# A centred head weight made on chip, the layers' result turned as it is, and the offset's row left in the tail

## The chip, the cores and the metric

The kernel runs on one core of one Trainium2 chip. Its time is the device time of one execution, in microseconds (us); the profile shows the same program in one execution of its own, as a span from the first to the last instruction. The engines are PE (TensorE: matmuls, with the weight loads kept apart as PEld), DVE (VectorE), ACT (ScalarE), POOL (GpSimd) and SP (SyncE, which here issues all DMAs). Each runs its own instructions in the order in which they are written and meets the others at semaphores.

## The reference

A small vision tower in three parts. Two images of 32 x 128 x 128 are cut into 256 patches each and embedded in 128 features. Two layers follow, each an attention with factored softmaxes and a feed-forward of 512 with GELU, all with layernorms. A last layernorm and a head of 128 x 192 give the tokens of the second and third parts, a linear attention and a feed-forward of 768 at width 192. What the change touches is the last norm and the head:

```
return _ln(x, lnf_g, lnf_b) @ head_w + head_b     # _ln: (x - mean) * rsqrt(var + eps) * g + b
...
h = h + attn(_layernorm(h))
h = h + ffn(_layernorm(h))
```

Written out for a token, h = rstd * ((x - mean) * g) @ head_w + (b @ head_w + head_b). The part (x - mean) can be taken on either side of the product: (x - mean) * g @ head_w equals x @ (g * head_w - m), where each row of m is the mean over the 128 features of g * head_w, since mean is a mean over the same features.

## The kernel before

All weights lie in SBUF and are loaded once by SP in a written order; nothing is tiled over DMA. A token tile is 128 tokens, and each image has two (`TILES`). Tensors x, h, xn, yT and so on exist once for each image (x0, x1), eight PSUM banks are shared under several names (`KB`, `QB`, `VB`, `SB_`, `CB`). The work of each engine is an order written out by hand in one block for each engine, so that what stands behind a waiting instruction waits too.

The start embeds image 0 and then image 1 (`conv`). Then come four steps s = 0 to 3, step s being the attention of layer s // 2 for image s % 2, with the feed-forward of the step before it folded in: on PE, the q, k and v products, `turn_k`, the feed-forward, `context`, `turn_q`, `context_out`, `attend`. After step 3 comes the tail: the head of image 0, the feed-forward of image 1's second layer (its norm is LN2(1)), and then the second and third parts of both images, interleaved.

A norm goes over five engines' turns: DVE takes moments (`bn_stats`, `bn_aggr` into mv), POOL makes rstd (`rsqrt`, L1356), DVE writes xn (`norm_apply`, L823), PE transposes xn into a bank, and ACT or DVE applies gain and offset on the way to SBUF as yT. The matrices are split in a high and a low part, so yT_lo (the rest of yT after rounding) is one more subtraction, `norm2_low`, on POOL (L1363) or, for the tail's LN2(1), on DVE (L853). `next_rsqrt` is `rsqrt` followed by `after_norm`, which holds POOL until DVE has written both tiles of xn.

The last norm, LNF, takes no rstd in xn: `normf_centre` (L830) on DVE writes x - mean, `turn_norm` transposes it, `normf` (L1200) on ACT multiplies by the gain, `head` (L501) multiplies by headw, and `h_from_head` (L967) on DVE multiplies by rstd and adds headb. headb is one row, repeated over 128 partitions: `offset_through_head` (L509) on PE, then `head_bias` (L836) on DVE. On PE the tail begins

```
attend(1, 1, 1)
turn_norm(0, LNF, CB)
offset_through_head()
head(0)
turn_norm(1, LN2(1), QB[0])
ff1_begin(1, 1)
ff1_end(1, 1)
turn_norm3(0, LN3, T3)
```

and `ff1_end` starts with a wait for image 1's yT_lo. LN3 is the norm ahead of the linear attention. `mix_masks` (L889) and `mix_sum` (L894) on DVE combine masks for the weights of the third part, in step 0; POOL first uses their result at `mix_fc(0)`, in step 2 (at 49.50 us of the profile).

Of the kernel before, what the change touches and what calls it, by code (L numbers as in the profile page):

```python
# [26 lines left out]
ALU = mybir.AluOpType  # L27
# [3 lines left out]
P = 128  # L31
# [4 lines left out]
D = 128  # L36
# [50 lines left out]
def build(nc, small, embed0, patches1, qkv_w, rest_w, rows, mix, fc_w, proj_w, head_w, aqkv_w, aout_w, out):  # L87
    with ExitStack() as ctx:
# [63 lines left out]
        headb = sb("headb", [P, E])  # L152

# [107 lines left out]
        headb_done, headb_ready = sem("headb_done"), sem("headb_ready")  # L261
# [27 lines left out]
        XN = {n: TILES * n for n in range(LN4 + 1)}  # L289
# [51 lines left out]
        def _(pe):  # L341
# [155 lines left out]
            def head(i):  # L497
                pe.wait_ge(loaded["head"], 16)
                pe.wait_ge(norm_ready[i], 2 * LAYERS + 1)
                for t in range(TILES):  # L500
                    mm = nc.tensor.matmul(HB[i][:, t * E:(t + 1) * E], yT[i][:, t * P:(t + 1) * P], headw[:],  # L501
                                          start=True, stop=True)
                mm.then_inc(head_done, 1)


            def offset_through_head():
                pe.wait_ge(loaded["head"], 16)
                offset = col("lnf_b").to_broadcast([P, P])
                nc.tensor.matmul(KB[1][:, 0:E], offset, headw[:], start=True, stop=True).then_inc(headb_done, 1)  # L509
# [147 lines left out]
            for t in range(TILES):  # L657
                conv(1, 13, KCONV, (t,))
            turn_q(0, 0, 0)
# [6 lines left out]
            for s in range(1, STEPS):  # L666
# [5 lines left out]
                pe.wait_ge(tile0_ready[i], 2 * l + 1)  # L672
                q_part(l, i, 0, "high")
# [39 lines left out]
                turn_q(l, i, 1)  # L713
                attend(l, i, 0)
# [4 lines left out]
            turn_norm(0, LNF, CB)  # L719
            offset_through_head()  # L720
            head(0)
# [15 lines left out]
            turn_norm(1, LNF, CB)  # L737
# [65 lines left out]
        def _(dve):  # L803
# [23 lines left out]
            def normf_centre(i):  # L827
                for t in range(TILES):
                    dve.wait_ge(moments[i], 2 * TILES * LNF + TILES + t + 1)
                    nc.vector.tensor_scalar(xn[i][:, t, 0:D], x[i][:, t, :], mv[i][:, t, 0:1], None,  # L830
                                            ALU.subtract).then_inc(xn_ready[i], 1)

            def head_bias():
                dve.wait_ge(headb_done, 1)
                dve.wait_ge(loaded["rows"], 16)
                nc.vector.tensor_tensor(headb[:], KB[1][:, 0:E], rows_sb[:, ROW["head_b"]:ROW["head_b"] + E],  # L836
                                        ALU.add).then_inc(headb_ready, 1)
# [125 lines left out]
            def h_from_head(i, t):  # L963
                dve.wait_ge(headb_ready, 1)
# [79 lines left out]
            mix_alpha()  # L1044

# [8 lines left out]
            for s in range(STEPS):  # L1054
# [26 lines left out]
                else:  # L1081
# [12 lines left out]
                    mix_masks()  # L1094
                context_scaled(l, i, 1)
                if s < STEPS - 1:
                    norm_apply(1 - i, LN1((s + 1) // 2), x[1 - i], D)
                else:
                    normf_centre(0)
                if s == 0:  # L1100
                    mix_sum()
# [9 lines left out]

            norm_apply(1, LN2(1), x[1], D)
            head_bias()
            for t in range(TILES):
                h_from_head(0, t)
            norm_stats(0, LN3, h[0], E, h_ready[0], 1, 1)
            norm2_low(1, 1)
            norm_apply(0, LN3, h[0], E)
# [9 lines left out]
            normf_centre(1)  # L1128
# [48 lines left out]
        def _(act):  # L1177
# [175 lines left out]
        def _(pool):  # L1353
# [227 lines left out]
```

## Time and profile before

| what | us |
|---|---|
| median of 3 runs | 122.61 |
| lowest and highest | 121.50, 123.34 |
| the profiled execution, its time | 121.18 |
| its span | 119.4 |
| PE busy in the span | 111.2 (93%) |
| DVE, ACT, POOL busy | 83.7, 64.8, 52.3 |
| span up to the head of step 1, steps 1 to 3 | 31.7; 14.2, 14.25, 14.05 |
| between the last step and the tail (74.2 to 80.5) | 6.3, of which PE busy 4.85 |

The profiled execution's time is 1.78 above its span, and it lies 1.43 under the median of the runs. Busy time of PE is that of matmuls in flight, so that a 93% busy PE need not be at its peak. TensorE's granted clock is full in all 40 slices of the page. A row of the timeline gives the start in us from the span's start, the length, the engine, the line of the kernel, what is written and read, and how many instructions of that kind were merged; the bracket at its end gives the idle time of the engine just ahead of it and what ended that.

### The profile page before, as it was taken

The page shows a single profiled execution, that of the slowest core. Times are in us where ns is not written, and L with a number is a line of the kernel's source. Part 1 is how long each engine was busy: PE and PEld are TensorE (multiplying, and loading weights), DVE is VectorE, ACT ScalarE, POOL GpSimd, SP SyncE. Part 2 cuts the span into 40 slices and gives each one's busy share as a digit, 9 for nine tenths or more (in the row PEclk, how much of TensorE's full clock was granted, in tenths as well). Part 3 has the DMA queues.
Part 4 walks back from the last instruction along what each step waited for, and adds up shares of the span by engine and source line. Part 5 has one row for each costly group of instructions (what it writes and reads, how often), then busy time and mean ns, then how long its engine had stood idle before and what let it go on. Part 6 is the DMA issues. An engine that isn't in the chain of part 4 may idle for free.

```text
span 119.4 us, 2459 instructions
## 1 busy us (share of the span) xinstructions
PE 111.2 (93%) x916; PEld 100.5 (84%) x916; DVE 83.7 (70%) x246; ACT 64.8 (54%) x148; POOL 52.3 (44%) x62
## 2 busy tenths in 40 slices
PE   6979999999999999999999999689958999999991
PEld 6969998987888989889897998379856979999990
DVE  5000376998999978999699998769896897264202
ACT  4000075464869967899679975257515283521520
POOL 0000108268049970697425999436806860022000
PEclk9999999999999999999999999999999999999999
DMA  3999999996900000000000000000000000000202
GB/s 106 341 409 419 397 367 414 419 407 192 370 2 0 0 5 3 0 0 5 0 0 0 0 5 0 5 0 0 5 0 0 0 0 0 5 0 0 66 0 66
DMA packets 4011, 11.97 MB, mean 100 GB/s; under 512 B 448, under 2 KB 1568, under 8 KB 4000
## 3 DMA queue, kind: packets, MB, share of 16 engines
q1 hardware_dynamic: 4000, 11.82, 26.2%
q8 instruction: 7, 0.11, 0.4%
q14 instruction: 4, 0.03, 0.1%
HBM read 11.43 MB, written 0.39 MB: 99 GB/s over the span
## 4 chain that ended last, share of the span: by engine, by line
PE 52%; DMA 12%; POOL 12%; DVE 7%; issue 6%; SPq 6%; ACT 3%; POOLq 0%; DVEq 0%
DMA restw<-in_rest_w 12%; PE bank L523 7%; PE bank L351 7%; PE bank L601 6%; PE bank L357 5%; PE bank L492 4%; PE bank L458 4%; PE bank L430 3%; PE bank L448 3%; POOL rstd L1356 3%; POOL aqkvw_lo L1417 2%; SPq L304 2%; PE bank L586 2%; SPq L310 2%; POOL qn L1375 2%
## 5 line engine op out<-in xcount | busy, mean ns | idle before, releaser
L1356 POOL TENSOR_TENSOR rstd<-mv,minus_half 128x2 f32<-128x2 f32 x14 | 10.6, 758 | 39.8 <-DVE mv L812 39.7
L1214 ACT ACTIVATE qkvw_hi<-qkvw 128x512 fp32r<-128x512 f32 x6 | 3.6, 626 | 12.9 <-DMA qkvw<-in_qkv_w 12.9
L1219 ACT ACTIVATE kexp<-bank,nkmax 128x256 f32<-128x256 f32 x16 | 7.4, 473 | 3.8 <-DVE nkmax L898 3.8
L1375 POOL TENSOR_TENSOR qn<-q,rqsum 128x512 f32<-128x512 f32 x8 | 8.3, 1042 | 2.4 <-DVE rqsum L921 2.4
L374 PEld LDWEIGHTS bank<-embed_sb 128*128 128x128 f32 x64 | 7.9, 200 | 1.0 <-DMA embed_sb<-in_embed 0.9
L601 PE MATMUL bank<-projw_raw,patches_sb 128*128 128x192 f32 x48 | 8.8, 326 | 0.0
L374 PE MATMUL bank<-embed_sb 128*128 128x128 f32 x64 | 8.1, 285 | 0.8 <-DMA embed_sb<-in_embed 0.8
L458 PE MATMUL bank<-cw,qT 128*128 128x128 f32 x64 | 8.8, 282 | 0.0
L374 PE MATMUL bank<-embed_sb,patches_sb 128*128 128x128 f32 x64 | 8.7, 278 | 0.0
L458 PEld LDWEIGHTS bank<-cw,qT 128*128 128x128 f32 x64 | 7.8, 192 | 0.8 <-issue 0.8
L374 PEld LDWEIGHTS bank<-embed_sb,patches_sb 128*128 128x128 f32 x64 | 8.1, 191 | 0.4
L1268 ACT ACTIVATE patches_sb<-bank,fcb 128x256 f32<-128x256 f32 x12 | 4.9, 471 | 6.3 <-PE bank L523 6.3
L492 PE MATMUL bank<-restw,hid 128*128 128x128 f32 x64 | 8.1, 280 | 0.0
L601 PEld LDWEIGHTS bank<-projw_raw,patches_sb 128*128 128x128 f32 x48 | 7.7, 190 | 0.0
L492 PEld LDWEIGHTS bank<-restw,hid 128*128 128x128 f32 x64 | 7.4, 192 | 0.2
L1417 POOL TENSOR_TENSOR qkvw_lo<-qkvw,qkvw_hi 128x512 fp32r<-128x512 f32 x5 | 6.3, 1281 | 2.9 <-DVE yT_lo L848 2.9
L1241 ACT ACTIVATE qT<-bank 128x512 f32<-128x512 f32 x8 | 4.8, 600 | 4.5 <-PE bank L448 4.5
L1247 ACT ACTIVATE hid<-bank,small_sb 128x256 f32<-128x256 f32 x16 | 6.3, 474 | 1.5 <-PE bank L351 1.5
L1370 POOL TENSOR_TENSOR xb<-x,rows_sb 128x256 f32<-128x256 f32 x8 | 5.9, 735 | 2.7 <-DVE xn L823 1.7
L357 PE MATMUL bank<-qkvw_hi,yT_lo 128*128 128x512 f32 x16 | 6.9, 432 | 0.0
L1179 ACT ACT_TABLE_LOAD x5 | 6.4, 1283 | 0.8 <-PEq L1573 0.7
L823 DVE TENSOR_SCALAR xn<-x,mv,rstd 128x128 f32<-128x128 f32 x16 | 4.8, 342 | 2.8 <-POOL rstd L1356 2.8
(152 smaller groups left out, 331.0 us busy)
## 6 DMA issues: line engine op xcount, KB each, us to landing
embed_sb<-in_embed SPq DMA_DIRECT2D x2, 768.0 KB, 6.6
restw<-in_rest_w SPq DMA_DIRECT2D x2, 768.0 KB, 15.1
patches_sb<-in_patches SPq DMA_DIRECT2D x2, 512.0 KB, 9.2
embed_sb<-in_embed SPq DMA_DIRECT2D x2, 384.0 KB, 8.0
qkvw<-in_qkv_w SPq DMA_DIRECT2D x3, 256.0 KB, 9.7
patches_sb<-in_patches SPq DMA_DIRECT2D x1, 768.0 KB, 12.0
qkvw<-in_qkv_w SPq DMA_DIRECT2D x1, 768.0 KB, 16.1
embed_sb<-in_fc_w SPq DMA_DIRECT2D x1, 768.0 KB, 6.2
```

The costliest lines, as they stand in the source:

```text
L351: mm = nc.tensor.matmul(dst, left(w, n), right(y, n), **ends(which, n, chunks))
L357: mm = nc.tensor.matmul(dst, left(y, n), right(w, n), **ends(which, n, chunks))
L374: mm = nc.tensor.matmul(EMB[i][t][:, 0:D], patches[:, t * P:(t + 1) * P], embed_sb[:, c, 0:D], start=(c == 0), stop=(c == KCONV - 1))
L458: mm = nc.tensor.matmul(VB[t][:, 0:D], qT[i][:, t, c * P:(c + 1) * P], cw[i][:, c, :], start=(k == 0), stop=(k == PAIRS - 1))
L492: mm = nc.tensor.matmul(banks[t][:, 0:D], hid[i][:, c, t * P:(t + 1) * P], ff2w(l, c), start=(c == 0), stop=(c == FC - 1))
L523: mm = nc.tensor.matmul(dst, left, right, start=(which == "high" and k == 0), stop=(which == "low" and k == len(order) - 1))
L601: mm = nc.tensor.matmul(QB[t][:, 0:E], hid3[i][:, c, t * P:(t + 1) * P], projw[:, c, :], start=(c == 0), stop=(c == HC - 1))
L1179: nc.scalar.activation(table_in[:], minus_half[:], func).then_inc(table_loaded, 1)
L1219: nc.scalar.activation(kexp[i][:, c, :], KB[c // 2][:, (c % 2) * TOKENS:(c % 2 + 1) * TOKENS], ACT.Exp, bias=nkmax[i][:, c:c + 1], accum_o ...
L1356: nc.gpsimd.tensor_tensor(rstd[i][:], mv[i][:, :, 1], minus_half[:], ALU.pow).then_inc(rstd_ready[i], 1)
L1375: nc.gpsimd.tensor_tensor(qn[i][:, t, :].rearrange("p (h d) -> p h d", h=HEADS), q[i][:, t, :].rearrange("p (h d) -> p h d", h=HEADS), rqs ...
L1417: nc.gpsimd.tensor_tensor(lo, raw, hi.bitcast(F32), ALU.subtract).then_inc(split_lo[name], 1)
```

## The change

There is a new buffer headc [128, 192], and a new column gain_mean = lnf_g / 128, made on DVE in the start. At the end of step 0 a new matmul on PE, `head_mean`, multiplies gain_mean, repeated over 128 columns, by headw and leaves the mean row in bank KB[0]; DVE's `head_centred` forms headc = headw * lnf_g - that row. `mix_masks` moves behind the `norm_apply` of step 0, `mix_sum` behind the one of step 1. The layers' result x is transposed without centring (`turn_x`), for image 0 inside the last step, ahead of its `attend`, for image 1 where the centred one was turned; `normf` on ACT is a plain copy. `head(0)` follows the last `attend` at once, and the offset's row comes behind it. On DVE, `head_bias` and both `h_from_head(0, t)` now stand ahead of `norm_apply(1, LN2(1))`, and `norm2_low(1, 1)` stands behind `norm_apply(0, LN3)`. On POOL `rsqrt(0, LNF)` moves ahead of two weight operations, and the second layer's bias of image 1 behind the rstd of LN3.

```diff
+            def head_mean():
+                pe.wait_ge(loaded["head"], 16)
+                pe.wait_ge(gain_mean_ready, 1)
+                pe.wait_ge(ktok_ready[0], 1)
+                nc.tensor.matmul(KB[0][:, 0:E], gain_mean[:].to_broadcast([P, P]), headw[:],
+                                 start=True, stop=True).then_inc(head_rows_done, 1)
+            def turn_x(i, dst):
+                for t in range(TILES):
+                    pe.wait_ge(x_new[i], TILES * (LAYERS - 1) + t + 1)
+                    mm = nc.tensor.transpose(dst[:, t * P:(t + 1) * P], x[i][:, t, :], ident)
+                mm.then_inc(turned[i], 1)
...
             for t in range(TILES):
                 conv(1, 13, KCONV, (t,))
+            head_mean()
             turn_q(0, 0, 0)
...
+                if s == 1:
+                    pe.wait_ge(head_rows_ready, 1)
                 q_part(l, i, 0, "high")
...
                 turn_q(l, i, 1)
+                if s == STEPS - 1:
+                    turn_x(0, CB)
                 attend(l, i, 0)
...
             attend(1, 1, 1)
-            turn_norm(0, LNF, CB)
+            head(0)
             offset_through_head()
-            head(0)
             turn_norm(1, LN2(1), QB[0])
...
-            turn_norm(1, LNF, CB)
+            turn_x(1, CB)
...
+            def head_centred():
+                dve.wait_ge(head_rows_done, 1)
+                nc.vector.scalar_tensor_tensor(out=headc[:], in0=headw[:], scalar=col("lnf_g"), in1=KB[0][:, 0:E],
+                                               op0=ALU.mult, op1=ALU.subtract).then_inc(head_rows_ready, 1)
...
-                nc.scalar.activation(yT[i][:], bankof[:, 0:TOKENS], ACT.Copy, scale=col("lnf_g")).then_inc(norm_ready[i], 1)
+                nc.scalar.activation(yT[i][:], bankof[:, 0:TOKENS], ACT.Copy).then_inc(norm_ready[i], 1)
...
             mix_proj_bias()
             normalise_q(1, 1, 1)
             add_bias(1, "out_b", 1, x_new[1], TILES)
+            rsqrt(0, LNF)
             aqkv_low_part(0)
             mix_fc_bias()
-            rsqrt(0, LNF)
-
-            next_rsqrt(1, LN2(1))
+
+            rsqrt(1, LN2(1))
+            next_rsqrt(0, LN3)
             add_bias(1, "ff2_b", 1, x_mid[1], TILES * LAYERS)
-            next_rsqrt(0, LN3)
```

Three places show how instructions stand (the lines in the second listing of each are those of the changed kernel). In the listings a row is one instruction or a run of equal ones: line, operation, what is written and read, and the columns. First DVE at the end of step 0, before and after (x1 is the embedded image 1, bank6 in the row of cw holds the attention's output weights times the context):

```order
L812 BN_AGGR mv1<-stats1 128x2 x2
L889 TENSOR_TENSOR weighted<-mix_sb,alpha 128x594
L948 TENSOR_SCALAR cw<-bank6,rksum0 128x128
L823 TENSOR_SCALAR xn1<-x1,mv1,rstd1 128x128 x2
L894 TENSOR_REDUCE coef<-weighted 128x66
L955 TENSOR_TENSOR x0<-bank4,xb0 128x128
L842 TENSOR_SCALAR yT1_hi<-bank6,small_sb 128x128
```

```order
L834 BN_AGGR mv1<-stats1 128x2 x2
L852 SCALAR_TENSOR_TENSOR headc<-headw,small_sb,bank0 128x192
L970 TENSOR_SCALAR cw<-bank6,rksum0 128x128
L845 TENSOR_SCALAR xn1<-x1,mv1,rstd1 128x128 x2
L911 TENSOR_TENSOR weighted<-mix_sb,alpha 128x594
L977 TENSOR_TENSOR x0<-bank4,xb0 128x128
L864 TENSOR_SCALAR yT1_hi<-bank6,small_sb 128x128
```

The masks' product made room for headc and went behind xn1, and the masks' sum left step 0; it stands behind xn0 of step 1.

Next PE from the last turn of q in step 3 to the first product of the feed-forward, before and after (bank4 and bank5 take the attention of the two tiles):

```order
L448 MATMUL bank3<-small_sb,qn 128x128 x4
L458 MATMUL bank4<-cw,qT 128x128 x4
L458 MATMUL bank5<-cw,qT 128x128 x4
L387 MATMUL bank7<-small_sb,xn0 128x128 x2
L509 MATMUL bank1<-headw,small_sb 128x192
L501 MATMUL bank0<-headw,yT0 128x192 x2
L387 MATMUL bank2<-small_sb,xn1 128x128 x2
L351 MATMUL bank7<-yT1_hi,ff1w1_hi 128x256
L351 MATMUL bank6<-yT1_hi,ff1w1_hi 128x256
```

```order
L451 MATMUL bank3<-small_sb,qn 128x128 x4
L526 MATMUL bank7<-small_sb,x0 128x128 x2
L461 MATMUL bank4<-cw,qT 128x128 x4
L461 MATMUL bank5<-cw,qT 128x128 x4
L504 MATMUL bank0<-headc,yT0 128x192 x2
L512 MATMUL bank1<-headw,small_sb 128x192
L390 MATMUL bank2<-small_sb,xn1 128x128 x2
L354 MATMUL bank7<-yT1_hi,ff1w1_hi 128x256
L354 MATMUL bank6<-yT1_hi,ff1w1_hi 128x256
```

The two transposes of image 0 went from behind the attention to ahead of it, and the head's two products ahead of the offset's row.

Last DVE from the close of LN2(1)'s moments to the first cast of LN3, before and after:

```order
L812 BN_AGGR mv1<-stats1 128x2
L823 TENSOR_SCALAR xn1<-x1,mv1,rstd1 128x128 x2
L836 TENSOR_TENSOR headb<-bank1,rows_sb 128x192
L967 SCALAR_TENSOR_TENSOR h0<-bank0,rstd0,headb 128x192 x2
L808 BN_STATS stats3_0<-h0 128x6 x2
L812 BN_AGGR mv0<-stats3_0 128x2 x2
L853 TENSOR_TENSOR yT1_lo<-yT1,yT1_hi 128x256
L823 TENSOR_SCALAR xn0<-h0,mv0,rstd0 128x192 x2
L859 CAST yT3_0_hi<-bank1 128x256
```

```order
L834 BN_AGGR mv1<-stats1 128x2
L858 TENSOR_TENSOR headb<-bank1,rows_sb 128x192
L989 SCALAR_TENSOR_TENSOR h0<-bank0,rstd0,headb 128x192 x2
L845 TENSOR_SCALAR xn1<-x1,mv1,rstd1 128x128 x2
L830 BN_STATS stats3_0<-h0 128x6 x2
L834 BN_AGGR mv0<-stats3_0 128x2 x2
L845 TENSOR_SCALAR xn0<-h0,mv0,rstd0 128x192 x2
L875 TENSOR_TENSOR yT1_lo<-yT1,yT1_hi 128x256
L881 CAST yT3_0_hi<-bank1 128x256
```

The offset row's sum and both tiles of h0 went ahead of xn1, and yT1_lo, for which the feed-forward's low products wait, went behind xn0.

## Rows read from the trace of the kernel before

**Rows 1.** Windows: stretch, length, busy us and instructions by engine, clock, DMA share, GB/s.

```profile
60.15:74.20 14.05, 14.04 (x136) 12.36 (x135) 13.37 (x36) 11.66 (x27) 10.73 (x13) 1.00 0.01 1
74.20:80.50 6.30, 4.85 (x29) 3.46 (x28) 4.31 (x17) 2.28 (x6) 2.62 (x5) 1.00 0.01 3
```

**Rows 2.** Timeline, end of step 0: start, length, engine, line, tiles, idle before.

```profile
27.43 0.60 PE L448 MATMUL bank<-small_sb,qn 128*128 128x128 f32 x4
...
28.05 0.43 PEld L441 LDWEIGHTS bank<-restw,ctxs 64*64 64x64 f32 x16 [0.26 <-DVE x L876]
...
28.54 0.74 DVE L889 TENSOR_TENSOR weighted<-mix_sb,alpha 128x594 f32<-128x594 uint8 x1
...
28.70 1.15 POOL L1356 TENSOR_TENSOR rstd<-mv,minus_half 128x2 f32<-128x2 f32 x1
...
29.66 0.37 ACT L1236 ACTIVATE cw<-bank,rksum 128x128 f32<-128x128 f32 x1 [0.25 <-DVE cw L948]
...
30.40 0.77 DVE L894 TENSOR_REDUCE coef<-weighted 128x66 f32<-128x594 f32 x1
...
31.08 0.28 DVE L955 TENSOR_TENSOR x<-bank,xb 128x128 f32<-128x128 f32 x1
...
31.73 0.19 PEld L357 LDWEIGHTS bank<-qkvw_hi,yT_hi 128*128 128x128 f32 x1 [0.16 <-DVE yT_hi L842]
```

**Rows 3.** DMA: the head weight's issue on the timeline, and its landing.

```profile
12.33 0.51 SPq L328 DMA_DIRECT2D headw<-in_head_w  x1
...
headw<-in_head_w SPq DMA_DIRECT2D x1, 96.0 KB, 15.2
```

**Rows 4.** Timeline, end of step 1.

```profile
44.20 0.60 DVE L823 TENSOR_SCALAR xn<-x,mv,rstd 128x128 f32<-128x128 f32 x2 [0.39 <-POOL rstd L1356]
...
45.20 0.29 DVE L955 TENSOR_TENSOR x<-bank,xb 128x128 f32<-128x128 f32 x1 [0.41 <-PE bank L458]
...
45.94 0.19 PEld L357 LDWEIGHTS bank<-qkvw_hi,yT_hi 128*128 128x128 f32 x1
```

**Rows 5.** Timeline and one line's summary, end of the last step.

```profile
72.17 1.62 DVE L830 TENSOR_SCALAR xn<-x,mv 128x128 f32<-128x128 f32 x2
...
72.39 1.91 PEld L458 LDWEIGHTS bank<-cw,qT 128*128 128x128 f32 x16 [0.20 <-issue]
...
74.54 0.49 PE L509 MATMUL bank<-headw,small_sb 128*128 128x192 f32 x2
...
75.18 0.20 DVE L812 BATCH_NORM_AGGREGATE mv<-stats 128x2 f32<-128x9 f32 x1
...
L509 PE MATMUL bank<-headw,small_sb x2: 326/327/328, 74.5 to 74.7; 128*128 128x192 f32 x2
```

**Rows 6.** Timeline, between the last step and the tail.

```profile
75.45 0.69 POOL L1356 TENSOR_TENSOR rstd<-mv,minus_half 128x2 f32<-128x2 f32 x1 [1.10 <-DVE mv L812]
...
76.18 0.60 DVE L823 TENSOR_SCALAR xn<-x,mv,rstd 128x128 f32<-128x128 f32 x2 [0.80 <-POOL rstd L1356]
...
76.69 0.35 DVE L836 TENSOR_TENSOR headb<-bank,rows_sb 128x192 f32<-128x192 f32 x1
...
77.08 0.74 DVE L967 SCALAR_TENSOR_TENSOR h<-bank,rstd,headb 128x192 f32<-128x192 f32 x2
...
78.50 0.38 DVE L853 TENSOR_TENSOR yT_lo<-yT,yT_hi 128x256 fp32r<-128x256 f32 x1
...
78.66 0.78 POOL L1356 TENSOR_TENSOR rstd<-mv,minus_half 128x2 f32<-128x2 f32 x1 [1.07 <-DVE mv L812]
...
78.93 0.19 PEld L351 LDWEIGHTS bank<-yT_lo,ff1w_hi 128*128 128x128 f32 x1 [0.24 <-DVE yT_lo L853]
...
79.47 0.67 DVE L823 TENSOR_SCALAR xn<-h,mv,rstd 128x192 f32<-128x192 f32 x2 [0.59 <-POOL rstd L1356]
```

**Rows 7.** Timeline, image 0's first minimum in the tail.

```profile
83.42 0.34 PE L523 MATMUL bank<-aqkvw_lo,yT_end 128*128 128x384 f32 x1
...
83.86 1.25 DVE L972 TENSOR_SCALAR q<-bank 128x384 f32<-128x384 f32 x2
```

More of the change, by code:

```diff
@@ L152, in build @@
         headb = sb("headb", [P, E])
+        gain_mean = sb("gain_mean", [P, 1])
+        headc = sb("headc", [P, E])
         def outw(l, p):
@@ L287, in build @@
         LOW.update({n: n + 1 for n in range(2 * LAYERS)})
-        XN = {n: TILES * n for n in range(LN4 + 1)}
+        XN = {n: TILES * n for n in range(LNF)}
+        XN.update({LN3: TILES * LNF, LN4: TILES * (LNF + 1)})
         HALVES = [SB_, CB]
@@ L500, in head @@
                 for t in range(TILES):
-                    mm = nc.tensor.matmul(HB[i][:, t * E:(t + 1) * E], yT[i][:, t * P:(t + 1) * P], headw[:],
+                    mm = nc.tensor.matmul(HB[i][:, t * E:(t + 1) * E], yT[i][:, t * P:(t + 1) * P], headc[:],
                                           start=True, stop=True)
@@ L508, in offset_through_head @@
                 offset = col("lnf_b").to_broadcast([P, P])
-                nc.tensor.matmul(KB[1][:, 0:E], offset, headw[:], start=True, stop=True).then_inc(headb_done, 1)
+                nc.tensor.matmul(KB[1][:, 0:E], offset, headw[:], start=True, stop=True).then_inc(head_rows_done, 1)
+            def head_mean():
[9 more added lines that the diff above has]
+                mm.then_inc(turned[i], 1)
             def parts3(i, which):
@@ L1044, in _ @@
             mix_alpha()
+            dve.wait_ge(loaded["small"], 16)
+            nc.vector.tensor_scalar(gain_mean[:], col("lnf_g"), 1.0 / D, None, ALU.mult).then_inc(gain_mean_ready, 1)
             for t in range(TILES):
@@ L1093, in _ @@
                     norm_stats(1, LN1(0), x[1], D, x_ready[1], 1, 1)
-                    mix_masks()
+                    head_centred()
                 context_scaled(l, i, 1)
@@ L1097, in _ @@
                     norm_apply(1 - i, LN1((s + 1) // 2), x[1 - i], D)
-                else:
-                    normf_centre(0)
                 if s == 0:
+                    mix_masks()
+                if s == 1:
                     mix_sum()
@@ L1110, in _ @@
                 close_moments(i, LN2(l), 1, D, 3)
+            head_bias()
+            h_from_head(0, 0)
+            h_from_head(0, 1)
             norm_apply(1, LN2(1), x[1], D)
-            head_bias()
             for t in range(TILES):
-                h_from_head(0, t)
-            norm_stats(0, LN3, h[0], E, h_ready[0], 1, 1)
+                add_moments(0, LN3, h[0], t, E, h_ready[0], t + 1)
+            for t in range(TILES):
+                close_moments(0, LN3, t, E, t + 1)
+            norm_apply(0, LN3, h[0], E)
             norm2_low(1, 1)
-            norm_apply(0, LN3, h[0], E)
             for c in range(EPC):
@@ L1127, in _ @@
                 close_moments(1, LNF, t, D, t + 1)
-            normf_centre(1)
             phi3_min(0, 0)
```

13 lines of the change are left out of this document (4 added, 9 removed).

## The prediction, made before the change was timed

> **What bounds the kernel now.** I read the windows by stage first: how long each stage is, and how much of it PE is busy. In the last step PE works 14.04 of 14.05 us; in the stretch between that step and the tail it works 4.85 of 6.30 [rows 1]. So inside the steps anything put on PE costs its full time unless PE waits just there, and anything taken off DVE, ACT or POOL is worth nothing unless a PE wait hangs on it. The 6.3 us stretch is different: there a chain through DVE, POOL and ACT is last. The timeline shows its links: the last moments of LN2(1) are closed at 75.18 [rows 5], POOL makes rstd from 75.45 to 76.14, DVE waits 0.80 us for it and writes xn1 from 76.18, and the feed-forward's low products start at 78.93 after a wait for yT_lo, which DVE wrote from 78.50 [rows 6]. That is the path on which the change must win or lose. The second thing to see is how wide DVE's gap ahead of 76.18 is, since the change puts work into it.
>
> **Step 0: a matmul added, a contact removed.** `head_mean` is one fp32 product of 192 columns, two passes. The offset's row is the same shape: passes of 0.326 us, two of them in 0.49 [rows 5], so that each takes a slot of about 0.16 and both 0.33. It stands ahead of the turn of q, which started at 27.43 [rows 2]. The head weight is issued at 12.33 and lands 15.2 later, at 27.5 [rows 3]; with the release, PE would start it at about 27.6. That is a wait of 0.15 and 0.33 of work, 0.48 in all. Behind it stand the turn of q and `context_out`, which in the trace waited 0.26 until 28.05 for image 1's x [rows 2]; it comes at about 28.35 instead. ACT's copy of q and its first two cw come 0.3 to 0.4 later for that, but ahead of the third cw ACT had waited 0.25, until 29.66, because DVE's cw stood behind the masks' product [rows 2]; so the third starts at about 29.7. headc takes that product's place: a product of 128x192 with one PSUM input, for which the nearest rows are headb, 0.35, and h, 0.74 for two [rows 6], against 0.74 for the masks. So the late start is eaten by the time that DVE gives back, and `attend` ends about 0.1 later.
>
> POOL's rstd beside the masks' product took 1.15, from 28.70 [rows 2], where the same operation takes 0.69 and 0.78 elsewhere [rows 6]: it was blocked until the product ended at 29.28. Now xn1 comes some 0.4 earlier, the masks' product behind it ends at about 30.7 instead of the sum's 31.17, and x0 is not held until 31.08. The wait of 0.16 at 31.73 [rows 2], the only PE time to be had here, then goes. 0.1 lost and 0.1 gained: I take 0 for the end of step 0. Bounds: -0.16, if `head_mean` hides wholly, and +0.35, if it hides only behind the 0.26 and the landing is no later.
>
> **Step 1: the masks' sum.** It takes 0.77 [rows 2] and now stands between xn0 (44.20) and x1 (45.20, after a wait of 0.41) [rows 4]. The next instruction starts 0.51 after such a pair of xn (76.18 to 76.69 [rows 6]), and x followed the sum's start by 0.68 (30.40 to 31.08 [rows 2]), 1.19 in all; so x1 comes at 45.4. From such an x it took 0.65 to the first product of the next step (31.08 to 31.73 [rows 2]), which gives 46.05 against 45.94 [rows 4]: +0.1. Bounds 0 and +0.36 (0.77 less the whole wait). POOL's first use of the sum is at 49.5, so nobody else waits.
>
> **Last step.** Both centrings took 1.62, since DVE stood behind POOL [rows 5]; a pair of the same size takes 0.60 [rows 6]. That looks like the prize, but it isn't: they are over at 73.79, and the loads of `attend` run until 74.30 [rows 5]; the chain goes on from its second tile. 0. `turn_x(0)` is two transposes in the 0.20 that PE waits ahead of `attend` [rows 5]: 0, and +0.2 if that wait doesn't cover it. ACT copies it while `attend` runs. What the ready yT0 does buy: head(0) starts where the loads of `attend` end, 72.39 + 1.91 = 74.30 [rows 5]. Four passes and the offset's two end at 74.3 + 5 x 0.16 + 0.33 = 75.5. All of it lies in PE's idle time, and is worth only what the freed time is worth.
>
> **Between the last step and the tail.** DVE is done with the moments at 75.38 [rows 5]. It then waits for the offset's row (75.55), takes 0.39 to the first h (76.69 to 77.08 [rows 6]) and some 0.66 for both (0.74 busy, of which the next instruction overlaps 0.08). That ends at 76.6, while rstd has been there since 76.14. So **xn1 goes from 76.18 to 76.6: +0.42**. DVE's gap was 0.80 and 1.05 us of work was put into it, starting 0.17 late. The transposes, ACT's two copies and the first products follow with the same +0.42. Bounds 0.25 (if the offset's row comes in time) and 0.6.
>
> Then yT1_lo. Before it was written as soon as DVE had closed LN3's moments. Now it stands behind xn0, which waits for LN3's rstd. From the first h to that rstd it took 78.66 - 77.08 = 1.58; xn1 now lies between (76.69 - 76.18 = 0.51), so rstd starts at 75.94 + 1.58 + 0.51 = 78.03, ends at about 78.8, and xn0 takes 0.67 [rows 6], of which yT_lo overlaps a little: it starts at 79.4 instead of 78.50. The products that wait for it are 0.43 later, as before: 79.83 against 78.93, **+0.90, of which 0.48 is this second term**. LN3's xn0 is ready 0.7 earlier, but PE turns it only after the feed-forward's low products, which stand ahead in its queue. Bounds of the second term: 0, if LN3's rstd comes in time, and +1.0 more by a block as in the last step's centring.
>
> **Tail.** The centring of image 1 goes too. What stood behind it, the minimum from 83.86, reads a product whose last pass ended at 83.42 + 0.34 = 83.76 [rows 7]: 0.06 is to be had, up to 0.39 if the modelled end of that matmul is late. After this PE and DVE hand work to each other as before, all of it shifted.
>
> **Sum.** 0 + 0.1 + 0 + 0.42 + 0.48 - 0.06 = +0.94 us. The profiled execution's 121.18 becomes 122.1; its span 119.4 becomes 120.3. The median of the runs shown, 122.61, lies 1.43 above that execution, and I put the sum on it: 123.5.
>
> **Rivals.**
> *Only the first term.* LN3's rstd is early enough, or ACT's yT1 late enough, for yT_lo to be held by nothing: +0.46, 123.1. Against it: without DVE's new order yT_lo would come 0.42 after 78.50, at 78.9, and DVE is at 79.4.
>
> *Not slower.* DVE's own work sets the tail's pace from 83.5 on, not PE's product, so that the centring gives back 0.39; step 0 gives its 0.16, and only +0.42 of the middle stays: about -0.1, 122.5. It decides if the minimum starts within 0.3 of the close of the moments. For it: no idle time stands ahead of 83.86 [rows 7]. Against it: the product's end fits as well.
>
> *A block at yT_lo.* POOL's bias of image 1 now starts when xn0 is written, just when DVE comes to yT_lo. If POOL is first, DVE stands as it did for the centring, whose pair took 1.62 instead of 0.60. I take 0.6 of that 1.0, POOL's operation being shorter: 124.1. The Trainium skill, page SBUF — State Buffer, section Who interferes with whom, says that a DVE instruction with two SBUF inputs and a GpSimd instruction that reads SBUF exclude each other and that issue order decides. yT_lo has two such inputs, so by the page this is possible and depends on a tenth of a microsecond; the rstd of 1.15 agrees with it.
>
> *Slower, beyond 2%: the head weight.* It is the last but two in SP's list and now stops PE in step 0. It lands at 27.5, right when it is wanted. Each us that it lands later than 27.6 delays the turn of q, `context_out` and all that follows; with 1.6 us, 125.2. Against it: the weights ahead of it in the same queue hold up the steps before as well, so a slower queue moves PE's place with it.
>
> **How the numbers follow.** Forecast 0.44, first term only 0.15, not slower 0.19, block 0.13, late weight 0.06, other 0.03. The predicted time is the forecast's, 123.5. The runs before lie 1.1 below to 0.7 above their median, so each case carries about that much. From 121.8 to 124.9 the range leaves out the late weight and the outer parts of the others. 2% is 2.45 us, about what a measurement of this kernel can tell from no change. Faster needs less than 120.2, for which no term is large enough: 0.02. Slower needs more than 125.1: 0.07. The rest, 0.91, is within.
>
> **What would show it.** In the changed profile: no long wait of PE for the head weight, the next product of step 1 within 0.2 of 31.7 and of step 2 within 0.3 of 46.0; head(0) at 74.4; xn1 at about 76.6 rather than 76.2, behind h; yT1_lo behind xn0 with PE idle ahead of the low products, which start near 79.9. I am wrong if the low products start before 79.2, if the minimum after LNF's moments moves by more than 0.1 against the product it reads, or if the head weight lands later than PE comes to it by over 0.3.

## The result and the profile after

The changed kernel takes **124.49 us** (median of 4 runs, 123.61 to 125.77) against 122.06 (median of 4, 121.15 to 123.34). The ratio is 1.0204, 95% interval 1.0138 to 1.027. The forecast was 123.5, its range 121.8 to 124.9. So the time lies in the range, but it is 1 us above the forecast and the increase is 2.4 us, where 0.94 was forecast. The changed kernel is slower; whether by more than 2% these executions don't settle. Why it is 2.4 and not 0.94 is what most of the experiments are about. Ratios here and below leave out the executions that took over 1.5% more than the fastest of their kernel, which in the experiments all had a lowered mean clock, so that a ratio is not that of the medians beside it.

The page of the changed kernel (the profiled execution took 125.32, its span 123.5) shows at once something that no row of before shows. Busy share and granted clock of PE in 40 slices of 3.09 us, in tenths:

```profile
PE   6979999999999999999999996599958999999992
...
PEclk9999999999999999999999999958997699999999
```

TensorE's granted clock leaves its full level twice behind the last step, each time behind a dip of PE. The windows say the same in 2 us stretches (length, then busy us of PE, PEld, DVE, ACT and POOL, then the granted clock). The changed kernel:

```profile
76.00:78.00 2.00, 0.52 (x3) 0.28 (x2) 1.89 (x7) 0.00 (x0) 0.69 (x1) 1.00 0.00 0
78.00:80.00 2.00, 1.08 (x5) 0.60 (x4) 1.20 (x6) 1.02 (x2) 0.69 (x1) 1.00 0.00 0
80.00:82.00 2.00, 1.66 (x9) 1.66 (x10) 0.28 (x1) 0.67 (x2) 1.97 (x4) 0.67 0.00 0
82.00:84.00 2.00, 2.00 (x11) 1.93 (x10) 1.37 (x4) 1.97 (x4) 1.22 (x2) 0.50 0.00 0
...
90.00:92.00 2.00, 0.75 (x9) 0.59 (x8) 2.00 (x8) 0.00 (x0) 0.00 (x0) 1.00 0.00 0
...
94.00:96.00 2.00, 2.00 (x10) 2.00 (x10) 1.27 (x3) 1.11 (x2) 1.19 (x2) 0.58 0.00 0
```

A clock of 0.50 is the lower of the two levels, 1.2 of 2.4 GHz. The kernel before in the same view, ahead of its tail and at its wait for kv:

```profile
76.00:78.00 2.00, 0.93 (x5) 0.40 (x3) 1.79 (x6) 0.80 (x2) 0.86 (x2) 1.00 0.02 4
78.00:80.00 2.00, 1.96 (x13) 1.55 (x13) 1.41 (x7) 0.51 (x2) 0.78 (x1) 1.00 0.00 0
...
88.00:90.00 2.00, 0.71 (x5) 0.57 (x4) 1.97 (x8) 0.00 (x0) 0.49 (x1) 1.00 0.00 0
90.00:92.00 2.00, 1.68 (x13) 1.25 (x12) 1.03 (x3) 1.22 (x3) 1.22 (x2) 1.00 0.00 0
```

From 76 to 80 PE was busy 0.52 + 1.08 of 4 us in the changed kernel and 0.93 + 1.96 before. The later idle stretch is the same in both (0.75 then 1.67, against 0.71 then 1.68), and only the changed kernel's profile shows a fall behind it. What the lower clock costs is seen on equal products. Here are the feed-forward's second products in the tail, 16 of them, by line (busy, mean ns of one, idle before), before and after:

```profile
L492 PE MATMUL bank<-restw,hid 128*128 128x128 f32 x16 | 1.9, 275 | 0.0
```

```profile
L495 PE MATMUL bank<-restw,hid 128*128 128x128 f32 x16 | 2.6, 329 | 0.0
```

**It is not in every execution.** For each execution the mean granted clock is known. In 67 executions of the kernel before, taken beside the experiments, 25 had the full clock throughout (median 121.39), 29 had a mean near 0.986 (122.87) and 13 one near 0.972 (124.20). In the profiles, an execution with one fall has 0.986 and one with two has 0.972, and I read the other executions by that. So the kernel before has falls too, only not in the execution that I read, and by these medians the first fall costs 1.48 us and the second 1.33. The changed kernel's four executions: two with one fall (median 123.63), two with two (125.54), none without.

Now the rows that answer to those of before. The end of step 0 [rows 2, 3]:

```profile
27.97 0.30 PEld L519 LDWEIGHTS bank<-headw,gain_mean 128*128 128x128 f32 x2 [0.38 <-DMA headw<-in_head_w]
...
28.71 0.37 DVE L852 SCALAR_TENSOR_TENSOR headc<-headw,small_sb,bank 128x192 f32<-128x192 f32 x1
28.87 0.70 POOL L1382 TENSOR_TENSOR rstd<-mv,minus_half 128x2 f32<-128x2 f32 x1
28.93 0.43 PEld L444 LDWEIGHTS bank<-restw,ctxs 64*64 64x64 f32 x16 [0.17 <-issue]
...
29.66 0.35 DVE L970 TENSOR_SCALAR cw<-bank,rksum 128x128 f32<-128x128 f32 x1 [0.58 <-PE bank L444]
29.93 0.59 DVE L845 TENSOR_SCALAR xn<-x,mv,rstd 128x128 f32<-128x128 f32 x2
...
32.14 0.19 PEld L360 LDWEIGHTS bank<-qkvw_hi,yT_hi 128*128 128x128 f32 x1
```

PE waits 0.38 for the head weight, `context_out` starts at 28.93, and step 1 at 32.14 instead of 31.73. The end of step 1 [rows 4], with the masks' sum ahead of x:

```profile
45.16 0.77 DVE L916 TENSOR_REDUCE coef<-weighted 128x66 f32<-128x594 f32 x1
45.84 0.28 DVE L977 TENSOR_TENSOR x<-bank,xb 128x128 f32<-128x128 f32 x1
...
46.56 0.19 PEld L360 LDWEIGHTS bank<-qkvw_hi,yT_hi 128*128 128x128 f32 x1
```

The stretch ahead of the tail [rows 5, 6]:

```profile
74.89 0.82 PE L504 MATMUL bank<-headc,yT 128*128 128x192 f32 x4
...
76.02 0.69 POOL L1382 TENSOR_TENSOR rstd<-mv,minus_half 128x2 f32<-128x2 f32 x1 [1.12 <-DVE mv L834]
76.07 0.36 DVE L858 TENSOR_TENSOR headb<-bank,rows_sb 128x192 f32<-128x192 f32 x1
76.47 0.74 DVE L989 SCALAR_TENSOR_TENSOR h<-bank,rstd,headb 128x192 f32<-128x192 f32 x2
77.12 0.59 DVE L845 TENSOR_SCALAR xn<-x,mv,rstd 128x128 f32<-128x128 f32 x2
...
79.28 0.67 DVE L845 TENSOR_SCALAR xn<-h,mv,rstd 128x192 f32<-128x192 f32 x2 [0.81 <-POOL rstd L1382]
79.87 0.42 DVE L875 TENSOR_TENSOR yT_lo<-yT,yT_hi 128x256 fp32r<-128x256 f32 x1
...
80.34 0.19 PEld L354 LDWEIGHTS bank<-yT_lo,ff1w_hi 128*128 128x128 f32 x1 [0.70 <-DVE yT_lo L875]
```

h stands ahead of xn1, LN3's xn ahead of yT_lo, and PE waits for yT_lo (its next weight load by 0.70). Last the first minimum of image 0 [rows 7]; DVE now waits for the product:

```profile
86.27 0.34 PE L541 MATMUL bank<-aqkvw_lo,yT_end 128*128 128x384 f32 x1
...
86.65 0.56 DVE L994 TENSOR_SCALAR q<-bank 128x384 f32<-128x384 f32 x1 [0.25 <-PE bank L541]
```

**Where the time went**, from these two traces. The loads of the start land 0.18 later (ACT's first use of the feed-forward weights at 23.40, not 23.22). From there to step 1's first product it takes 8.74 instead of 8.51: +0.23. Step 1 takes 14.42 instead of 14.21: +0.21, step 2 14.15 instead of 14.22: -0.07. From step 3's start to the low products it takes 19.63 instead of 18.77: +0.86. From the low products' start to the first q product of the tail (PEld L541; L523 before) 4.76 instead of 3.32: +1.44, with the clock down in it. From that row to the end 38.40 instead of 37.15: +1.25, with the second fall in it. Sum 4.10, and the spans differ by 123.5 - 119.4 = 4.1. Two thirds of it lie where the clock is down.

### The profile page after: what moved, and what is told of

It is laid out like the page before. It is cut to its first block, busy times and chain, and to the rows that moved or that the text cites. A ratio compares the mean times of both kernels' runs of the same rounds, so it can differ in the third digit from the quotient of the medians.

```text
span 123.5 us, 2463 instructions
## 1 busy us (share of the span) xinstructions
PE 114.0 (92%) x918; PEld 104.0 (84%) x918; DVE 82.5 (67%) x244; ACT 64.5 (52%) x148; POOL 51.8 (42%) x62
## 4 chain that ended last, share of the span: by engine, by line
PE 61%; DMA 12%; SPq 9%; DVE 6%; issue 5%; POOL 4%; POOLq 0%; DVEq 0%
DMA headw<-in_head_w 12%; PE bank L354 9%; PE bank L541 7%; PE bank L360 7%; PE bank L461 6%; PE bank L495 6%; PE bank L619 6%; PE bank L451 3%; PE bank L604 3%; PE bank L433 3%; POOL rstd L1382 3%; PE bank L423 2%; SPq L307 2%; SPq L329 2%; PE bank L444 2%
## 5 line engine op out<-in xcount | busy, mean ns | idle before, releaser
L1382 POOL TENSOR_TENSOR rstd<-mv,minus_half 128x2 f32<-128x2 f32 x14 | 10.1, 719 | 44.9 <-DVE mv L834 44.8
L495 PE MATMUL bank<-restw,hid 128*128 128x128 f32 x64 | 8.7, 293 | 0.0
L495 PEld LDWEIGHTS bank<-restw,hid 128*128 128x128 f32 x64 | 8.2, 207 | 0.2
L360 PE MATMUL bank<-qkvw_lo,yT_hi 128*128 128x512 f32 x16 | 6.5, 405 | 0.0
```

Source lines behind the costliest of these rows:

```text
L360: mm = nc.tensor.matmul(dst, left(y, n), right(w, n), **ends(which, n, chunks))
L495: mm = nc.tensor.matmul(banks[t][:, 0:D], hid[i][:, c, t * P:(t + 1) * P], ff2w(l, c), start=(c == 0), stop=(c == FC - 1))
L1382: nc.gpsimd.tensor_tensor(rstd[i][:], mv[i][:, :, 1], minus_half[:], ALU.pow).then_inc(rstd_ready[i], 1)
```

## The experiments

`fill(n)` in them is n fp32 products of the constant `ones` with itself, 192 columns, into a bank that is free at that place; they only keep PE busy. Ratios are against the kernel before on the same chip.

**1. The changed kernel with PE kept busy in the stretch ahead of the tail.**

```diff
             offset_through_head()
+            fill(4)
             turn_norm(1, LN2(1), QB[0])
+            fill(2)
             ff1_begin(1, 1)
+            fill(2)
             ff1_end(1, 1)
```

> The changed kernel with eight fp32 matmuls of 128x192 that nobody reads put into the three places where PE waits behind the last step (4 ahead of the turn of LN2(1), 2 behind it, 2 ahead of the low products). The order of DVE, ACT and POOL stays. Theory 1 (the clock): the changed kernel's 125.32 us execution lost 1.4 us near 80.6 to 84.1 and 1.4 near 94.4 to 97.6, where TensorE's granted clock was at half, and the first loss follows the idle PE of 76 to 80. With PE kept at work there the clock stays full up to 84, and the time falls by 1.4 us at least against the changed kernel: 122.0 to 123.0. Theory 2 (the clock falls for a reason of its own, whatever PE did before): the clock falls as before and the time stays at 123.6 to 125.8.

122.29 (10 executions), ratio 1.003 (0.9989 to 1.007), and all ten at the full clock. Its windows:

```profile
76.00:78.00 2.00, 1.82 (x12) 1.41 (x11) 1.97 (x7) 0.01 (x1) 0.57 (x1) 1.00 0.00 0
78.00:80.00 2.00, 1.90 (x11) 1.43 (x10) 1.20 (x6) 1.01 (x2) 0.81 (x2) 1.00 0.00 0
80.00:82.00 2.00, 2.00 (x18) 1.86 (x17) 0.48 (x3) 1.04 (x3) 2.00 (x4) 1.00 0.00 0
...
90.00:92.00 2.00, 1.41 (x9) 1.02 (x9) 1.42 (x6) 0.83 (x2) 1.01 (x1) 1.00 0.00 0
```

The low products start as late as in the changed kernel: 19.62 after step 3's start. So up to there the fill moves nothing but the clock. Behind it, against this trace, the changed kernel's two stretches with the clock down are longer by 1.61 (4.76 against 3.15 up to the first q product) and 1.44 (38.40 against 36.96 from there to the end). The change thus has two costs that can be told apart. At the full clock it is +0.90 (122.29 against 121.39 of before's executions at the full clock). The rest of the 2.4 goes with the falls of the clock, and is added up further down.

**2. DVE's old order in the changed kernel:** xn1 ahead of headb and h, yT_lo ahead of LN3's xn.

```diff
+            norm_apply(1, LN2(1), x[1], D)
             head_bias()
             h_from_head(0, 0)
             h_from_head(0, 1)
-            norm_apply(1, LN2(1), x[1], D)
...
+            norm2_low(1, 1)
             norm_apply(0, LN3, h[0], E)
-            norm2_low(1, 1)
```

> The changed kernel with DVE's old order behind the last step: xn1 of LN2(1) ahead of the offset row's sum and h0, and yT1_lo ahead of LN3's xn0. Theory 1 (the two moves of DVE cost 0.37 and 0.49 us, and the longer PE wait that they make drops the clock): low products 0.85 earlier against the last step, a full clock to 84, 121.7 to 122.5 us, within 0.7 above the kernel before. Theory 2 (what is lost lies in step 0, step 1 and the clock, and not in DVE's order): 123.5 or more.

122.44, ratio 1.0039 (0.9994 to 1.0084). The low products start 18.79 after step 3's start (before 18.77): both terms go with the order. Of 11 executions 5 were at the full clock (122.18), four had one fall (122.82), two had two. One thing doesn't fit: the four with one fall lie at before's 122.87, as the trace's terms say, but the five at the full clock lie 0.79 above before's 121.39. No profile shows one of these, and it stays open.

The expectation of a full clock up to 84 was not met in the profiled execution (two falls, 124.70):

```profile
76.00:78.00 2.00, 0.86 (x4) 0.28 (x2) 1.16 (x5) 0.00 (x0) 0.69 (x1) 1.00 0.00 0
78.00:80.00 2.00, 1.23 (x6) 0.86 (x7) 1.69 (x7) 1.02 (x2) 0.53 (x1) 1.00 0.00 0
80.00:82.00 2.00, 2.00 (x11) 1.96 (x11) 0.67 (x2) 1.18 (x3) 1.22 (x3) 0.50 0.00 0
```

PE is busy 2.09 of the 4 us here, and 2.89 before (2.88 when both are counted from step 3's start), though the low products come at the same place in the step. From 14.1 after step 3's start to the low products PE idles 1.44 us before, 1.90 in run 2 and 2.74 in the changed kernel. So 0.84 of the 1.30 more goes with DVE's order. The other 0.46 is work that the change took forward: image 0's two turns lie in the last step now, and the head's products follow it at once, so that PE waits for xn1 in one piece of 1.12, where before it waited 0.33 for ACT's yT and 0.33 for xn1. DVE's order explains the path, but not all of the idle stretch.

**3. Only yT_lo moved back.**

```diff
+            norm2_low(1, 1)
             norm_apply(0, LN3, h[0], E)
-            norm2_low(1, 1)
```

> The changed kernel with only one move of DVE undone: yT1_lo ahead of LN3's xn0; the offset row's sum and h0 stay ahead of xn1. Theory 1: low products 0.5 us earlier than in the changed kernel. If the shorter wait also keeps the clock, 122.0 to 123.0 us; if the clock still falls once, 123.2 to 124. Theory 2 (yT1_lo stood behind a POOL operation rather than behind xn0): less than 0.2 us and no change of the clock.

123.17, ratio 1.0093 (1.0036 to 1.0151); one of 10 executions at the full clock (121.41), six with one fall. The timeline:

```profile
79.11 0.43 DVE L875 TENSOR_TENSOR yT_lo<-yT,yT_hi 128x256 fp32r<-128x256 f32 x1 [0.72 <-ACT yT L1221]
...
79.59 0.19 PEld L354 LDWEIGHTS bank<-yT_lo,ff1w_hi 128*128 128x128 f32 x1
```

yT_lo now waits for ACT alone, and the low products come 18.96 after step 3's start. So h ahead of xn1 costs 0.19 by itself, and yT_lo's place the other 0.67 of the 0.86. PE still waits from the last step on for xn1, and the clock still falls.

**4. The head weight loaded earlier,** ahead of the masks in SP's list.

```diff
+            sp.dma_start(headw[:], head_w).then_inc(loaded["head"], 16)
             sp.dma_start(mix_sb[:], mix).then_inc(loaded["mix"], 16)
...
-            sp.dma_start(headw[:], head_w).then_inc(loaded["head"], 16)
```

> The changed kernel with the head weight's load two places earlier in SP's list, ahead of the masks and the second layer's rest. Theory 1 (PE's wait for it costs 0.2 to 0.4 us at the end of step 0): the weight lands about 2 us earlier, PE does not wait for it, step 1 starts 0.2 to 0.4 earlier, and the time falls by as much, 123.3 to 125.5, the clock falling as before. Theory 2 (the wait is covered by the wait for the embedded image 1, so that only the matmul itself costs): step 1 starts within 0.1 of the changed kernel's 32.14, no change in the time.

123.9 (4 executions), ratio 1.0145 (1.004 to 1.025). The ends of step 0:

```profile
27.69 0.30 PEld L519 LDWEIGHTS bank<-headw,gain_mean 128*128 128x128 f32 x2
...
31.88 0.19 PEld L360 LDWEIGHTS bank<-qkvw_hi,yT_hi 128*128 128x128 f32 x1
```

No wait stands at the head weight's product, and step 1 starts 8.29 after the loads' landing, against 8.74 in the changed kernel and 8.51 before. So the wait of 0.38 cost 0.45, and without it step 0 gains 0.22, which I put down to the masks' move; no run moves the masks alone. None of the four was at the full clock, so this part alone doesn't settle the time.

**5. The early part of the change alone:** headc, its product, the masks' moves, on the old tail (with the centring left as it was).

```diff
             for t in range(TILES):
                 conv(1, 13, KCONV, (t,))
+            head_mean()
             turn_q(0, 0, 0)
...
-                    mix_masks()
+                    head_centred()
...
                 if s == 0:
-                    mix_sum()
+                    mix_masks()
+                if s == 1:
+                    mix_sum()
```

> The kernel before with one part of the change alone: gain_mean, the mean row's product ahead of the first turn of q, headc in the masks' place, masks and sum moved as in the change, head with headc, plain copy. The tail's orders stay as before, centring included (it changes nothing, since headc takes the mean out again). Theory 1 (step 0 costs 0.2 to 0.3 us, the sum in step 1 0.2): 121.8 at full clock against 121.4 of the kernel before, and full clock about as often as the kernel before has it, in half of the executions. Theory 2 (these early parts are what makes the clock fall later): rarely or never at full clock.

123.9 (4 executions), ratio 1.0109 (1.0015 to 1.0202). By its trace step 0 costs +0.14 (8.65 after the landing) and step 1 +0.21; the low products come 18.79 after step 3's start, as before. Two executions had one fall, two had two. In the profiled one it is the late one:

```profile
88.00:90.00 2.00, 0.71 (x9) 0.58 (x8) 2.00 (x9) 0.00 (x0) 0.00 (x0) 1.00 0.00 0
90.00:92.00 2.00, 1.68 (x10) 1.11 (x11) 1.26 (x4) 1.08 (x2) 1.08 (x2) 0.94 0.00 0
92.00:94.00 2.00, 2.00 (x8) 1.92 (x9) 1.26 (x3) 1.11 (x2) 0.92 (x1) 0.50 0.00 0
```

If it fell as the kernel before does (42 of 67), four of four would come up 15 times in 100, so this is no evidence that the early part brings falls. The run can't tell. What it does show is that PE's work in the stretch doesn't decide: 0.71 and 1.68 busy here, with a fall, are the kernel before's figures, without one.

**6. The kernel before with PE kept busy there,** five products in all.

```diff
             offset_through_head()
+            fill(1)
             head(0)
+            fill(1)
             turn_norm(1, LN2(1), QB[0])
+            fill(2)
             ff1_begin(1, 1)
+            fill(1)
             ff1_end(1, 1)
```

> The kernel before with five fp32 matmuls of 128x192 that nobody reads in PE's waits behind the last step (1, 1, 2 and 1). Theory 1 (the kernel before loses time to the clock in half of its executions too, 1.25 us for one fall and 2.8 for two, by the same mechanism): full clock in all executions, 121.3 to 121.8, and no executions above 122. Theory 2 (the kernel before's slower executions have another cause): the same spread as now, 121.0 to 124.5.

121.64, ratio 0.995 (0.9894 to 1.0006); nine of 10 at the full clock, where the kernel before was in 25 of 67. The fill gives the kernel before what its falls cost it, 1.1 us between the medians (121.64 against 122.75), though by the ratio, which leaves out most of its executions with falls, no gain is certain.

**7. The changed kernel mended, no fill:** the head weight early, `turn_q` ahead of `head_mean`, headb, then xn1, then h, and yT_lo ahead of LN3's xn (the load as in run 4, yT_lo as in run 3).

```diff
-            head_mean()
             turn_q(0, 0, 0)
+            head_mean()
...
             head_bias()
+            norm_apply(1, LN2(1), x[1], D)
             h_from_head(0, 0)
             h_from_head(0, 1)
-            norm_apply(1, LN2(1), x[1], D)
```

> The changed kernel mended in four places: the head weight loaded two places earlier, the mean row's product behind the first turn of q, on DVE only the offset row's sum ahead of xn1 (it fits the wait for rstd) and both h0 behind it, yT1_lo ahead of LN3's xn0. No filling matmuls. Theory 1 (all of the +0.94 sits in those places but for 0.2 to 0.3): 121.6 to 121.8 at full clock, and full clock in some executions only, since PE waits between the last step and the tail longer than in the kernel before. Theory 2 (the longer idle stretch comes from the early head and turn, and nothing brings it back): no execution at full clock.

122.42, ratio 1.005 (0.9994 to 1.0105). The low products come 18.57 after step 3's start, 0.20 earlier than before, and step 1 starts 8.28 after the landing. Still none of 10 executions was at the full clock; seven had one fall (122.23, against 122.87 of before's with one). The profiled one's is behind the wait for kv:

```profile
78.00:80.00 2.00, 1.99 (x14) 1.62 (x14) 1.19 (x4) 0.72 (x3) 1.04 (x2) 1.00 0.00 0
...
88.00:90.00 2.00, 1.12 (x8) 0.96 (x8) 1.53 (x7) 0.22 (x1) 0.92 (x1) 1.00 0.00 0
90.00:92.00 2.00, 1.68 (x9) 1.22 (x7) 1.28 (x4) 1.07 (x3) 1.07 (x2) 0.70 0.00 0
92.00:94.00 2.00, 2.00 (x9) 2.00 (x7) 0.66 (x2) 0.89 (x2) 1.03 (x1) 0.50 0.00 0
```

So the mend took away all the added time (at an equal number of falls it is 0.6 under the kernel before), but not the falls.

**8. The same with fill ahead of the tail** (3, 2 and 1 products at the places of the first experiment).

> The same mended kernel with six matmuls that nobody reads in PE's waits behind the last step (3, 2 and 1). Theory 1: full clock always, 121.6 to 121.9, which is within 0.3 of the kernel before with such matmuls. If the earlier h0 and the centring that is gone are worth something once nothing is late, it comes below it, at 121.2. Theory 2 (filling delays what it should cover): 122 or more at full clock.

121.5 (4 executions), ratio 0.9894 (0.9773 to 1.0015). Three at the full clock (median 120.9), one with a fall near 91, so the expected full clock in all was missed by one.

**9. The same, and fill at the wait for kv as well.**

```diff
             context3(0)
+            fill(4)
             context_out3(0)
             turn_q3(0)
+            fill(1)
```

> The mended kernel with its six matmuls that nobody reads behind the last step, and five more in the tail: four ahead of the product of the output weights, where PE waits 1.3 us for kv, and one ahead of the turn of image 1's LN3. The mended kernel with the first six only fell to half clock from 90.6 to 94, after that wait. Theory 1 (each idle stretch can cost one fall, and filling both leaves none): full clock in all executions, 120.7 to 121.3, 0.2 to 0.5 below the kernel before with the same filling. Theory 2 (the second fall has nothing to do with that wait): falls at 90 to 94 as often as without.

121.39, ratio **0.9939** (0.9905 to 0.9973), 12 of 12 at the full clock:

```profile
88.00:90.00 2.00, 2.00 (x15) 1.79 (x14) 2.00 (x9) 0.00 (x0) 0.15 (x1) 1.00 0.00 0
90.00:92.00 2.00, 2.00 (x15) 1.39 (x13) 0.99 (x4) 1.08 (x2) 1.22 (x2) 1.00 0.00 0
```

**10. The kernel before with both fills.**

> The kernel before with both sets of matmuls that nobody reads, five behind the last step and five in the tail. Theory 1: full clock in all executions, 121.1 to 121.7, the same as the kernel before has when its clock never falls. Theory 2 (the late set delays kv's use): 122 or more.

121.42, ratio **0.9932** (0.9896 to 0.9967), 12 of 12 at the full clock or within 0.002 of it. With the clock held, the mended change and the kernel before can't be told apart by their times: 121.39 against 121.42; the 0.2 to 0.5 expected between them is not there. The fill itself takes a part of what the mend gave: in the mended kernel the low products come 18.57 after step 3's start without fill and 18.76 with it (run 9), in the kernel before 18.77 and 18.78. Their traces, both at the full clock, do differ: from the loads' landing to the end of the span it takes 119.7 - 23.91 = 95.79 mended and 119.5 - 23.24 = 96.26 before with fill. The landing itself lies between 23.18 and 23.94 in the profiles, a spread larger than this gain. Both kernels beat the two of the comparison, and what they share is the clock.

**11. The changed kernel with the late fill only.**

> The changed kernel with only the five late matmuls; the long wait of PE behind the last step is left as it is. Theory 1 (that wait costs one fall in nearly every execution, the kv wait the second): one fall near 80 to 84 in all executions, none at 90 to 97, 123.4 to 123.9, no executions at 125. Theory 2 (the falls come from the kv wait alone): full clock, 122.3.

124.02, ratio 1.0164 (1.0116 to 1.0211). None of 6 was at the full clock; four had one fall (123.56) and two had two, where one in each was expected. In the profiled one it is the early one:

```profile
78.00:80.00 2.00, 1.13 (x4) 0.65 (x5) 1.20 (x7) 1.02 (x2) 0.69 (x1) 1.00 0.00 0
80.00:82.00 2.00, 1.50 (x10) 1.29 (x10) 0.88 (x3) 0.28 (x1) 1.37 (x3) 0.91 0.00 0
82.00:84.00 2.00, 2.00 (x12) 1.93 (x11) 1.06 (x3) 1.98 (x5) 1.83 (x3) 0.50 0.00 0
...
90.00:92.00 2.00, 2.00 (x17) 1.98 (x17) 2.00 (x7) 0.33 (x1) 0.00 (x0) 1.00 0.00 0
```

So behind the idle stretch ahead of the tail the clock falls with the later one filled. Together with the first run: fill ahead of the tail takes the falls away, fill behind it doesn't.

## Why the prediction was right and where it was wrong

**The terms of the sum** came out at +0.90 by the executions at the full clock (run 1), or +0.82 by run 1's trace without the loads' landing (0.18 + 0.20 - 0.05 + 0.85 - 0.17 - 0.19), where +0.94 was forecast. The total is close, partly because errors cancel. That the measured time lies in the range is in part luck: the forecast stood on a median of 122.61, which a fourth execution made 122.06. On 122.61 the measured ratio would have given 125.1, above the range. By step, from the changed kernel's own trace:

- *Step 0, forecast 0:* +0.23. PE started the head weight's product at 27.97, not 27.6, after a wait of 0.38; it came just beyond the 0.3 at which I had called myself wrong. `context_out` came at 28.93, not 28.35: 0.18 of that is the loads, and of the wait of 0.26 that was to absorb a part of the product, 0.17 was still there. Loaded earlier, the same step is -0.22 (run 4), a little beyond my lower bound of -0.16. A second error: rstd was indeed freed (0.70, no longer 1.15), but xn1 came at 29.93, not 0.4 earlier, since in DVE's queue the cw stands ahead of it and waited 0.58 for PE.
- *Step 1, forecast +0.1:* +0.21. x started 0.68 behind the sum's start, as forecast. But xn came 0.03 later in the step, and from x to the product it took 0.72, not 0.65.
- *turn_x and the last step, forecast 0:* held. head(0) ran from 74.89, 14.18 after step 3's start.
- *The low products, forecast +0.90:* +0.86. The split was wrong: 0.42 and 0.48 were forecast for xn1 behind h and for yT_lo behind xn0, and the runs show 0.19 and 0.67. xn1 did come 0.39 later in the step, but yT_lo did not hang on it alone. Before, ACT had written yT1 by 78.22, and yT_lo started 0.28 later, behind DVE's moments of h0. In run 3 yT1 is there at 79.08, and yT_lo starts at 79.11. So in run 3 yT_lo starts only 0.14 later in the step (18.48 against 18.34), and the low products 0.19. The mechanism, two queue positions on DVE, is shown by runs 2 and 3.
- *The tail, forecast -0.06, to -0.39:* -0.36 in run 1's trace, -0.17 of it ahead of the tail's first q product. The size is near the far bound, but 0.17 of it comes before the centring's place, so that the centring has at most the other 0.19. In the changed kernel DVE waits 0.25 for the product of its first minimum, so it is PE, not DVE, that is late there.

The rows for yT1: ACT's write in the kernel before and in run 3.

```profile
77.67 0.55 ACT L1195 ACTIVATE yT<-bank,small_sb 128x256 f32<-128x256 f32 x1
```

```profile
78.52 0.56 ACT L1221 ACTIVATE yT<-bank,small_sb 128x256 f32<-128x256 f32 x1
```

Of the signs, the starts of steps 1 and 2 missed theirs: 32.14 and 46.56, 0.44 and 0.56 past 31.7 and 46.0, where 0.2 and 0.3 were allowed; 0.18 of each is the loads.

**The rivals.** Only the first term: no, 0.67 hangs on the second. Not slower: its gain in the tail came, its gain in step 0 didn't. A block at yT_lo: no, yT_lo started 0.59 behind xn0's start as in a free queue, took 0.42; POOL's bias started 0.16 behind it, and it was the bias that grew, to 0.84. The head weight late: in part, 0.38 of a wait.

**What was missed** is in one clause of the tail's part: "after this PE and DVE hand work to each other as before, all of it shifted". The added wait of PE lies beside an idle stretch that was there already, and the granted clock fell behind it, so that products which I had only shifted took 329 ns instead of 275. Part of the longer idle stretch is work that the change took forward (run 2); I had noted that it "lies in PE's idle time" and priced it at nothing. The forecast read that stretch as "6.3 us, of which PE busy 4.85" and asked only who is late. It didn't ask what PE's being idle does to what follows. The same view had a hint: the profiled execution, with a clock of 1.00 in every slice, was 1.43 below its kernel's median. I put the difference on the sum without asking for its cause. It is about the price of one fall, which 42 of 67 of before's later executions had; the clocks of the three behind that median are not on record.

That the change brings falls doesn't rest on four executions: runs 4 and 11 leave the stretch ahead of the tail as the change has it, and none of their 10 was at the full clock either. At before's share of 42 in 67, 14 of 14 would come up about once in 700 times.

How the 2.4 us of the medians come about: +0.90 on the path, and the changed kernel's falls (1 or 2 in each execution, 1.5 at the mean) against before's 0.82 at the mean, (29 + 2 x 13) / 67. That is 0.68 more at 1.4, +0.95. The sum is 1.85, which leaves 0.6. Four executions on either side can be off by that: before's medians beside the experiments, over 19 to 25 executions each, were 122.02, 122.75 and 122.87, against 122.06 over four here.

The Trainium skill, page TensorE: Matmul & The Clock Gate, in Part 1, The HAM clock gate, says that the array's clock is 1.2 or 2.4 GHz by how busy PE has lately been, and that the look at it isn't tied to the start of the kernel. The traces agree with the first: 0.50 behind idle stretches. That the same program has no, one or two falls fits the second, but no run here shows it.

**What stays open.** Fill ahead of the tail alone kept the clock in 22 of 24 executions (runs 1, 6, 8), though PE still idles at the wait for kv. Without it the mended kernel fell there in the profile, and in 10 of 10 executions it fell somewhere (run 7). So a fall at the wait for kv hangs on something ahead of it as well, and no run says on what. Nor is there a profile of an execution of the kernel before with a fall, so that where it has them is not shown. Run 2's executions at the full clock are 0.8 slower than its terms say, and the mended kernel's 0.47 by the trace doesn't show in its median (run 10); both are unexplained.

## What to carry to other kernels

Where PE has idle stretches behind a long dense phase, cost a wait that is added to them twice: once on the path, once for the granted clock behind it. Work taken forward out of such a stretch makes it idler too. And look at whether the executions' times come in groups before you call their spread noise. A profile with the full clock in each slice tells nothing of the executions without it; compare its time to the median first. A few products on spare operands in PE's idle time were worth more here (0.6 to 0.7% by the ratios, 1.2% between the medians) than the restructuring, mended or not.

## What the runs showed of the hardware

One fall of the granted clock costs 1.3 to 1.6 us here, and two executions have a mean clock that reads as three (0.958 and 0.957, at 126.02 in run 3 and 125.09 in run 7). Behind an idle stretch with PE busy 1.60 of 4 us the clock fell to 0.50 for some 3 us; behind one with 2.39 of 4 it fell in one profile (run 5) and not in another (before). Five to eleven products of 192 columns, put where PE waited (in the mended kernel at a price of 0.19 us), kept it full in 46 of 48 executions of the five kernels that had some ahead of the tail; with fill at the later place alone none of 6 kept it (run 11). On POOL the rstd of two columns took 1.15 us beside the masks' product on DVE, and 0.70 at the same place once that product had been moved.
